# Eight VectorE scans per chunk, recorded with the chunk's build, in a gated delta-rule layer

## The reference, cut to what matters

```python
q, k, v = (silu(x @ W) for W in (Wq, Wk, Wv)); log_f = log_sigmoid(x @ Wf1 @ Wf2)
beta = sigmoid(x @ Wbeta) * 2.0;  k = k / sqrt(sum(k * k) + EPS)
k_ = -beta[..., None] * k
# two steps of the state S per token: (log_f, k_ * exp(log_f), k, 0, 0) and (0, k_, k, k, v)
S = exp(g)[..., None] * S + a_t[..., None] * (b_t @ S) + k_t[..., None] * v_t
o = q_t @ S                       # at every second step
y = rmsnorm(o * sigmoid(x @ Wog1 @ Wog2)) * norm_w @ Wo
```

## Time and profile before

| | us |
|---|---|
| timed runs, median of 2 | 6597.96 (6582.65 to 6613.27) |
| the profiled execution | 6485.18 |
| its span (slowest core, core 1) | 6483.6 |
| spans of the 8 cores | 6454.2 to 6483.6 |
| busy: TensorE matmul / VectorE / ScalarE / POOL | 4113.4 / 2423.1 / 1897.1 / 351.3 |
| mean granted TensorE clock, core 1 | 0.737 |

### The profile page before, as it was taken

One profiled execution on the slowest core, in us unless ns is written; L12 is line 12 of the kernel. 1 busy time (PEld: TensorE's weight loads), 2 busy tenths in 40 slices (PEclk: granted clock), 3 DMA queues, 4 the chain that ended last, 5 costly groups with the idle time before them and its releaser, 6 DMA issues.

```text
span 6483.6 us, 87888 instructions; the slowest of 8 cores (6454.2 to 6483.6 us)
## 1 busy us (share of the span) xinstructions
PE 4113.4 (63%) x30797; PEld 2750.1 (42%) x30797; DVE 2423.1 (37%) x5219; ACT 1897.1 (29%) x3443; POOL 351.3 (5%) x344
## 2 busy tenths in 40 slices
PE   0056666666656566656665666666565738878888
PEld 0034444343534343434343444435353525555555
DVE  0143535353534354444444353535353411111111
ACT  0042333333232323232323333332323212222222
POOL 0010101010000000000001010101000000000000
PEclk9977677676676666676766767766666668888889
DMA  9511010101010201010110101010101030100000
GB/s 110 126 41 46 20 46 20 46 20 65 1 65 1 65 1 66 9 57 28 39 43 24 46 20 46 20 46 21 65 1 46 1 124 30 36 27 27 27 27 27
DMA packets 92517, 255.91 MB, mean 39 GB/s; under 512 B 11531, under 2 KB 14252, under 8 KB 89270
## 3 DMA queue, kind: packets, MB, share of 16 engines
q1 hardware_dynamic: 91382, 229.33, 10.7%
q0 software_dynamic: 704, 20.97, 2.8%
HBM read 233.48 MB, written 58.72 MB: 45 GB/s over the span
## 4 chain that ended last, share of the span: by engine, by line
PE 49%; DVE 20%; ACT 11%; issue 8%; DMA 7%; another core or an unknown queue 2%; SPq 1%; DVEq 1%; ACTq 0%; POOL 0%; POOLq 0%
PE PB L84 49%; DVE Pm_sb L84 6%; DVE X_sb L84 3%; DVE Lam L84 2%; ACT U_sb L84 2%; DVE lncol L84 2%; DMA Wbuf<-wbf_Wk 1%; ACT L84 1%; ACT v_bf L84 1%; SPq L84 1%; DVE Bm L84 1%; DVE scrA L84 1%; DMA x_sb<-x2scratch 1%; ACT yT_bf L84 1%
## 5 line engine op out<-in xcount | busy, mean ns | idle before, releaser
L84 ACT CAST U_sb<-PB 128x512 bf16<-128x512 f32 x1024 | 598.8, 585 | 1387.5 <-PE PB L84 1347.0
L84 DVE CAST X_sb<-PB 128x512 bf16<-128x512 f32 x640 | 439.4, 687 | 652.3 <-PE PB L84 652.3
L84 PE MATMUL PB<-U_sb,consts 128*128 128x128 bf16 x3584 | 605.5, 255 | 108.4 <-ACT U_sb L84 108.3
L84 PE MATMUL PB<-U_sb,Pm_sb 128*128 128x128 bf16 x3584 | 599.6, 256 | 43.6 <-DVE Pm_sb L84 41.0
L84 DVE CAST Pm_sb<-PB 128x512 bf16<-128x512 f32 x768 | 519.3, 683 | 170.2 <-PE PB L84 170.0
L84 PE MATMUL PB<-lnT,Wbuf 128*128 128x256 bf16 x2048 | 351.2, 341 | 255.2 <-DMA Wbuf<-wbf_Wk 159.0
L84 PE MATMUL PB<-X_sb,Pm_sb 128*128 128x128 bf16 x2048 | 224.2, 240 | 410.5 <-DVE Pm_sb L84 410.5
L84 PEld LDWEIGHTS PB<-U_sb,consts 128*128 128x128 bf16 x3584 | 416.2, 116 | 138.1 <-issue 129.2
L84 PE MATMUL PB<-W_bf,hfm 128*128 128x512 bf16 x2048 | 444.6, 379 | 12.7 <-ACT hfm L84 12.7
L84 PEld LDWEIGHTS PB<-U_sb,Pm_sb 128*128 128x128 bf16 x3584 | 417.7, 117 | 63.6 <-issue 61.4
L84 PEld LDWEIGHTS PB<-lnT,Wbuf 128*128 128x128 bf16 x2048 | 243.3, 120 | 364.0 <-issue 294.6
(11 more groups left out here) (148 smaller groups left out, 6553.4 us busy)
## 6 DMA issues: line engine op xcount, KB each, us to landing
Wbuf<-wbf_Wv SPq DMA_DIRECT2D x128, 256.0 KB, 5.0
Wbuf<-wbf_Wo SPq DMA_DIRECT2D x128, 256.0 KB, 4.7
Wbuf<-wbf_Wq SPq DMA_DIRECT2D x15, 2048.0 KB, 8.0
Wbuf<-wbf_Wk SPq DMA_DIRECT2D x120, 256.0 KB, 5.8
wbf_w<-w POOLq DMA_DIRECT2D x2, 8192.0 KB, 78.8
x_sb<-x SPq DMA_DIRECT2D x32, 512.0 KB, 4.8
x2scratch<-x_sb SPq DMA_DIRECT2D x32, 512.0 KB, 2.9
W_bf<-wbf_w SPq DMA_DIRECT2D x64, 256.0 KB, 6.8
```

What stands on the lines that cost most here:

```text
L84: inst = getattr(e, fname)(*args, **kw)
```

## The change

There are two edits, and a smaller mask that makes room for the first.

- k-norm loop: `KtP[0]`, `sqrow` and `sqbf` become pairs that alternate with j. The order of the calls stays.
- Scans: the 32 scans ahead of `chunk_build_elem(0)` go; the function itself now begins with the 8 scans of its own chunk, on VectorE. Since the function is also what is recorded into `pending`, the scans of chunks 1, 2 and 3 are now the first 8 operations of the lists of chunks 0, 1 and 2, which have 54 operations, and nper is 8.
- `consts2` keeps 256 instead of 512 columns of the mask c_maskKQ (only 256 are read).

```diff
-        consts2, tconsts2 = mk(ctx, "consts2", [64, 1024], BF16)
+        consts2, tconsts2 = mk(ctx, "consts2", [64, 768], BF16)
...
+            sqrowB, tsqrow2 = mk(ctxA, "sqrowB", [1, 512], F32)
+            sqbfB, tsqbf2 = mk(ctxA, "sqbfB", [1, 512], BF16)
...
-                dma(consts2[:, 512:1024], c_maskKQ.ap(), writes=[tconsts2], dsem="DC")
+                dma(consts2[:, 512:768], c_maskKQ.ap()[:, 0:256], writes=[tconsts2], dsem="DC")
...
                     for j in range(4):
-                        b.op("S", "activation", KtP[0][0][:],
+                        b.op("S", "activation", KtP[j % 2][0][:],
                              k_f32[:, j * 512:(j + 1) * 512], AF.Square,
-                             reads=[tk], writes=[KtP[0][1]])
+                             reads=[tk], writes=[KtP[j % 2][1]])
                         bank, tb = PS[4 + j % 2]
                         b.op("T", "matmul", bank[0:1, :], onescol[:],
-                             KtP[0][0][:], start=True, stop=True,
-                             reads=[tones, KtP[0][1]], writes=[tb])
-                        b.op("S", "activation", sqrow[0:1, :],
+                             KtP[j % 2][0][:], start=True, stop=True,
+                             reads=[tones, KtP[j % 2][1]], writes=[tb])
+                        srow = sqrow if j % 2 == 0 else sqrowB
+                        tsrow = tsqrow if j % 2 == 0 else tsqrow2
+                        sbfr = sqbf if j % 2 == 0 else sqbfB
+                        tsbfr = tsqbf if j % 2 == 0 else tsqbf2
+                        b.op("S", "activation", srow[0:1, :],
                              bank[0:1, :], AF.Ln, bias=epsc[0:1, 1:2],
-                             reads=[tb, tepsc], writes=[tsqrow])
-                        b.op("S", "activation", sqbf[0:1, :],
-                             sqrow[0:1, :], AF.Exp, scale=-0.5,
-                             reads=[tsqrow], writes=[tsqbf])
+                             reads=[tb, tepsc], writes=[tsrow])
+                        b.op("S", "activation", sbfr[0:1, :],
+                             srow[0:1, :], AF.Exp, scale=-0.5,
+                             reads=[tsrow], writes=[tsbfr])
...
-                    for hh in range(H):
-                        for cc in range(NCH):
+                    _beng = ["P"]
+                    def chunk_build_elem(cc):
+                        for hh in range(H):
                             b.op("V", "tensor_tensor_scan",
                                  Lam4[:, hh, cc, :], lam4[:, hh, cc, :],
                                  lam4[:, hh, cc, :], 0.0, ALU.add, ALU.bypass,
                                  reads=[tlam], writes=[tLam])
-                    _beng = ["P"]
-                    def chunk_build_elem(cc):
```

More of the change, by code:

```diff
@@ L571, in build_program @@
                     for j in range(4):
-                        b.op("S", "activation", KtP[0][0][:],
+                        b.op("S", "activation", KtP[j % 2][0][:],
                              k_f32[:, j * 512:(j + 1) * 512], AF.Square,
-                             reads=[tk], writes=[KtP[0][1]])
+                             reads=[tk], writes=[KtP[j % 2][1]])
                         bank, tb = PS[4 + j % 2]
                         b.op("T", "matmul", bank[0:1, :], onescol[:],
-                             KtP[0][0][:], start=True, stop=True,
-                             reads=[tones, KtP[0][1]], writes=[tb])
-                        b.op("S", "activation", sqrow[0:1, :],
+                             KtP[j % 2][0][:], start=True, stop=True,
[5 more added lines that the diff above has]
+                        b.op("S", "activation", srow[0:1, :],
                              bank[0:1, :], AF.Ln, bias=epsc[0:1, 1:2],
-                             reads=[tb, tepsc], writes=[tsqrow])
-                        b.op("S", "activation", sqbf[0:1, :],
-                             sqrow[0:1, :], AF.Exp, scale=-0.5,
-                             reads=[tsqrow], writes=[tsqbf])
+                             reads=[tb, tepsc], writes=[tsrow])
+                        b.op("S", "activation", sbfr[0:1, :],
+                             srow[0:1, :], AF.Exp, scale=-0.5,
+                             reads=[tsrow], writes=[tsbfr])
                         b.op("T", "matmul", bank[:], onescol[0:1, 0:1].broadcast_to((1, 128)),
-                             sqbf[0:1, :], start=True, stop=True,
-                             reads=[tones, tsqbf], writes=[tb])
+                             sbfr[0:1, :], start=True, stop=True,
+                             reads=[tones, tsbfr], writes=[tb])
                         b.op("V", "scalar_tensor_tensor",
```

## The result

The changed kernel takes 6680.9 us (median of 11 runs, 6674.0 to 6849.4), the kernel before 6589.2 us (10 runs, 6486.2 to 6632.9). The ratio is 1.0255, with a 95% interval of 1.0188 to 1.0321: slower by 2.6%, and whether by more than 2% the interval leaves open. The ratio compares undisturbed runs alone (it comes out as the mean of nine, 6686.7 us, over that of two of the kernel before, 6486.2 and 6555.2 us); the chip has a slower state in which most of the kernel before's ten runs fell, so the two medians by themselves would give 1.014. The profiled executions are 190.7 us apart (6675.9 against 6485.2). The forecast was 6801 us in a range of 6640 to 6890, and +203 us between profiled executions.

A forecast was written before the change was run, and what follows sets the result against it. VectorE's 32 scans were taken to bound each macro's front, with TensorE idle until gate_bf. Chunks +22.3 less front 9.6 gave +12.7 us per macro, x 16 = +203; added to the median 6598: 6801 us, range 6640 to 6890.

The forecast's parts named there:

- The front: Start of each macro, up to gate_bf: 24 of 32 VectorE scans leave, so 9.6 us less per macro.
- The k-norm loop: Paired buffers in the k-norm loop gain 0, since ScalarE's order stays and no engine waited for a buffer.
- rival B: The k-norm loop does overlap through its new buffers, 63 us less: 6738 us; 4% chance.
- Scans free in the chunks: In chunks 0 to 2 the 8 moved scans, 3.05 us, fit VectorE's idle time before the X_sb cast: no cost.
- The first stall: Level 1, chunks 0 to 2: U_sb copies wait behind lexc and eX; +5.3, +4.4, +4.1, sum 13.8 us per macro.
- The second stall: Level 2, chunks 0 to 2: TensorE's Am transposes wait for VectorE; +1.7 us each, 5.1 us per macro.
- the clock: TensorE's clock may fall to 1.2 GHz in levels 1 and 2, raising the chunks' cost from 18.9 to 25.7 us.
- the middle that I took: Chunks' cost per macro taken as 22.3 us, between 18.9 with the clock unchanged and 25.7 with it lowered.
- my upper end: Chunks cost 25.7 us per macro if TensorE runs at 1.2 GHz in levels 1 and 2; +258 us in total.
- rival C: Chunks: only the first stall, no second, table load hidden; +47 us, 6645 us; 15% chance.
- A: Chunks: the chain behind the scans stays hidden, so the kernel is faster, -154 us, 6444 us; 7% chance.
- D: Chunks 0 to 2: the clock stays low for four more levels each; +461 us, up to 7059 us; 8% chance.

The follow-up runs named there:

- e3: The changed kernel with 6 instead of 8 listed operations in level 2, so Am's two transposes stand in level 3; ratio 1.0131, timed median 6610 us.
- e9, e10: A follow-up kernel; the text given does not say which change or measured time belongs to this label.

## Why the prediction was right, step by step

- **The front, -9.6 us.** Measured -9.8 to gate_bf, and -0.4 from there to T_sb. Nothing that I had called free turned up: ScalarE's first eX came 0.49 us after its last sigbc copy.
- **The k-norm loop, 0.** Measured -0.2 us, and the kernel with the buffers alone has 1.0002. The argument from ScalarE's order holds; rival B falls, and the reordered loop shows that the order was what it lacked.
- **Scans free in the chunks.** They end at 2306.49, and the X_sb cast starts at 2306.71; KQ-U0 is unchanged (4.62 to 4.74). Right.
- **The first stall, +5.3, +4.4, +4.1.** Measured 9.85 - 4.73 = 5.1, 4.1 and 4.2. The table load went where I had put it, in the open behind lexc, and chunk 0 pays for it.
- **The second stall and the clock.** For U1-U2 at 1.2 GHz my terms give 2.45 + 5.05 = 7.5 us, and it is 7.44 in each chunk; at 2.4 GHz they give 5.9, and the filled kernel has 5.96 (2653.96 to 2659.92, first U matmuls of its chunk 1 above). Here the middle that I took was wrong in its reason, and it came close by luck. In all three chunks the U matmuls of levels 1 and 2 ran at 0.50, which is what my upper end, 25.7 us, assumes; the clock recovers only later in level 2. What was measured is 23.0, against a forecast of 22.3. Level by level the upper end has 13.8 us to U1, where 13.4 was measured, 8.7 for U1-U2, where it was 7.7, and 3.2 for U2-U3, where it was 3.1. Most of the miss in U1-U2 is the baseline: in the one macro that I had looked at the three chunks took 5.30, 4.24 and 4.24 us there, and on average over all macros the kernel before takes 4.77, 4.83 and 4.97, 0.8 us more in sum. The other 1.2 us came back in the opening and behind U3, where I had put 0. So two errors, the clock at half its price and a baseline read in a single macro, nearly cancelled. A mean over all macros would have shown the second beforehand.
- **The sum.** +12.3 us per macro against +12.7, and 191 us between the profiled executions against 203. The timed forecast of 6801 us is 120 us above the 6681 measured, and nearly all of that is the baseline: 113 us because I added the 203 to the median of two timed runs, 6598, and not to the profiled 6485, and 12 us from the forecast of the change, less 5 us by which the changed kernel's median stands above its profiled execution. Eight of the changed kernel's eleven timed runs lie within 12 us of its profiled execution, and in the later rounds the kernel before had medians of 6521, 6501 and 6541 us. So 6681 lies outside my own range for the mechanism, 6747 to 6856, though the mechanism held, and it lies inside 6640 to 6890 only because I had widened that for rival C. That is luck too.
- **Slips of arithmetic.** The stretch to the end of the third eX is 6.35 us in the rows and 6.25 in the sum; C's 2.9 x 16 is 46, not 47. Neither matters.
- **Rivals.** A is shown to need exactly what it lacked: lexc ahead of the chunk. With that it gives 0.9703 where A had -154 us, 0.977. C had no second stall and a hidden table load. The changed kernel has both in the open (3.70 us before the transposes, and the load at 2308.04), and e3 shows that the second stall was worth 7.4 us per macro; with it gone the kernel is still slower, 1.0131. D didn't happen: from level 3 on the times are the old ones within 0.7 us.

## What to carry to other kernels

Idle time on the engine that gets the moved work is not enough: ask what starts when it is done, and in whose queue that stands ahead of what. Here 24 scans cost nothing by themselves, gave 9.8 us in front, and cost 23 us through what came behind them: 13.4 through exponentials that stood ahead of a copy, and the rest through two transposes that stood ahead of the level's products and through the lower clock. The same scans in an earlier gap cost nothing in the chunks, and 1.1 us between gate_bf and T_sb (9.96 against 8.90). Work that feeds a chain goes as early as an idle engine allows, not to where the chain is; a recorded list that grows by eight entries moves everything behind them; and two buffers didn't help a loop whose calls were still written one round after the other.

## What the runs showed of the hardware that I had not expected

The rest of the kernel, the same code in all runs, took between 1292 and 1376 us on the slowest cores of the profiled executions, and it goes with the granted clock there. 500 us of the feed-forward part in the kernel before, the changed one, and the one with the scans only, on the slowest core, and then in that last kernel again, same execution, on core 7 (the columns as above):

```profile
5700.00:6200.00 500.00, 417.87 (x2665) 271.58 (x2662) 86.66 (x241) 115.60 (x252) 0.00 (x0) 0.89 0.09 30
```
```profile
5700.00:6200.00 500.00, 409.45 (x2685) 273.58 (x2684) 87.08 (x246) 127.74 (x278) 0.00 (x0) 0.88 0.08 29
```
```profile
5700.00:6200.00 500.00, 419.01 (x2469) 261.70 (x2468) 80.99 (x220) 110.17 (x240) 0.00 (x0) 0.82 0.08 27
```
```profile
5700.00:6200.00 500.00, 414.88 (x2706) 274.64 (x2707) 83.98 (x227) 127.26 (x276) 0.00 (x0) 0.89 0.08 27
```

0.82 against 0.88, and 2469 matmuls in that time instead of 2685. It isn't the program: in that execution the rest took 1371 and 1375 us on cores 0 and 1, and 1289 to 1302 us on the other six, which ran the same code. The long rests of the other executions stand on pairs of cores too (6 and 7 in e3, e9 and e10). What sets it isn't settled by these runs. It is why a kernel's total can differ by over 1% from another's whose macro period is the same, and why the periods above decide more than the totals.

A wait of TensorE also costs more than its length: with the first wait filled each of three chunks is 1.4 us shorter ((312.49 - 308.38) / 3), though from U0 to U1 it takes as long or longer, and the clock between U1 and U2 is 0.95 to 1.00 instead of 0.51 to 0.61.
